# Weight preparation woven into the first two image rows, and a reordered setup, in a fused convolution, expert and recurrence kernel

## The reference

```python
# block 1: involution, 7x7 kernels made from the normalised pixel itself
w = relu(bn(conv1_w @ n1)); w = conv2_w @ w + conv2_b       # 4 groups x 49 taps
out1[c,h,w] = sum_k w[g(c),k,h,w] * patch[c,k,h,w]
# block 2: 16 experts, the top two weighted by their gates
out2 = sum_e dispatch[e] * w3[e] @ (silu(w1[e] @ n2) * (w2[e] @ n2))
# block 3: 3x3 convolution whose 64x64x9 kernel is a sum of low-rank products
y1 = conv(n3, S1s) @ U1s;  y2 = conv(n3, U2s) @ S2s;  out3 = (y1+y2)/12 + bias
# block 4: a recurrence over all 3136 pixels of an image, in row order
i,o = sigmoid(U x_t + V h); g = tanh(U x_t + V h); c = h*c + i*g; h = o*tanh(c)
```

## Time and profile before

| | us |
|---|---|
| median of three runs (4188.93 to 4189.55) | 4189.06 |
| the profiled execution | 4187.62 |
| its span, first to last instruction | 4184.9 |
| setup, to the first matmul of row 0 | 34.4 |
| rows 0 and 1 | 29.7 and 29.4 |
| preparation after row 1, after row 3 | 11.2 and 17.9 |
| from the first recurrence step to the end (3136 steps) | 3933.4 |

### The profile page before, as it was taken

The page is one execution under the profiler, slowest core; times in us unless marked ns, Lnnn a source line. Parts: engine busy times, 40 slices in busy tenths (PEclk is TensorE's granted clock), DMA queues, the critical chain, the costliest instruction groups (busy, mean ns, idle before and its releaser), DMA issues.

```text
span 4184.9 us, 135477 instructions
## 1 busy us (share of the span) xinstructions
PE 3651.3 (87%) x35548; PEld 2427.1 (58%) x35548; DVE 3452.3 (82%) x21845; ACT 2620.1 (63%) x11611; POOL 2187.3 (52%) x3228
## 2 busy tenths in 40 slices
PE   3788989898989898989898989898989898988887
PEld 2565656565656555656565655555656565655555
DVE  5678888888888888888888888888888888887777
ACT  1256666666666666666666666666666666666665
POOL 6565555555555555555554555555555555552222
PEclk9875555555555555555555555555555555555555
DMA  4000000000000000000000000000000000000000
GB/s 71 1 2 1 1 1 1 1 1 1 1 1 1 1 1 1 1 1 1 1 1 1 1 1 1 1 1 1 1 1 1 1 1 1 1 2 1 1 1 1
DMA packets 44543, 11.08 MB, mean 3 GB/s; under 512 B 39914, under 2 KB 44011, under 8 KB 44491
## 3 DMA queue, kind: packets, MB, share of 16 engines
q1 hardware_dynamic: 42378, 10.05, 1.5%
q10 hardware_dynamic: 2112, 0.46, 0.1%
HBM read 7.29 MB, written 3.21 MB: 3 GB/s over the span
## 4 chain that ended last, share of the span: by engine, by line
PE 56%; ACT 18%; DVE 18%; issue 7%; POOL 1%; SPq 0%; DVEq 0%; POOLq 0%; DMA 0%; ACTq 0%
PE GATES L1195 22%; ACT O L664 10%; PE YB L1022 8%; ACT G L661 8%; DVE HR L850 8%; DVE O L847 8%; PE YB L1162 5%; PE TAPB L1009 5%; PE DB L1130 5%; PE DB L1003 3%; PE H1B L1049 1%; PE H2B L1049 1%; PE TAPB L1054 1%; PE TAPB L1171 1%; PE GATES L992 1%
## 5 line engine op out<-in xcount | busy, mean ns | idle before, releaser
L661 ACT ACTIVATE G<-GATES 128x12 f32<-128x12 f32 x3136 | 572.7, 183 | 1254.6 <-PE GATES L1195 1198.0
L1195 PEld LDWEIGHTS GATES<-HR,VN 128*128 128x128 f16 x9408 | 496.6, 108 | 1306.1 <-DVE HR L850 1252.3
L1195 PE MATMUL GATES<-HR,VN 128*128 128x4 f16 x9408 | 758.9, 175 | 392.4 <-DVE HR L850 257.2
L842 DVE TENSOR_TENSOR_SCAN CT<-G,CT 128x12 f32<-128x12 f32 x3136 | 587.4, 187 | 306.6 <-ACT G L661 266.3
L664 ACT ACTIVATE O<-G 128x16 f32<-128x16 f32 x3136 | 690.1, 220 | 98.9 <-ACT G L661 0.2
L847 DVE RECIPROCAL O<-O 128x4 f32<-128x4 f32 x3136 | 567.4, 181 | 197.5 <-ACT O L664 0.9
L1195 PE MATMUL GATES<-H,VW 128*128 128x4 f16 x9408 | 712.9, 170 | 0.0
L850 DVE TENSOR_TENSOR_SCAN HR<-O,CT 128x20 f16<-128x20 f32 x3136 | 614.5, 196 | 4.6
L859 DVE SCALAR_TENSOR_TENSOR CT<-HIST,CT 128x4 f32<-128x4 f32 x3136 | 522.3, 167 | 108.8
L1022 PE MATMUL YB<-HD,W 128*64 128x112 f32 x3840 | 600.1, 411 | 2.4 <-DVE HD L751 2.2
L509 POOL TENSOR_TENSOR HD<-VV,DBS 128x448 f32<-128x448 f32 x392 | 444.3, 1133 | 271.3 <-ACT DBS L653 270.9
(11 more groups left out here) (236 smaller groups left out, 5588.2 us busy)
## 6 DMA issues: line engine op xcount, KB each, us to landing
out_dram<-OUT SPq DMA_DIRECT2D x112, 28.0 KB, 2.0
X<-in_x_dram SPq DMA_DIRECT2D x4, 672.0 KB, 13.4
STG<-in_L_ffn_w_dram SPq DMA_DIRECT2D x4, 512.0 KB, 8.0
U<-in_L_conv_U2s_dram SPq DMA_DIRECT2D x1, 972.0 KB
W<-in_L_ffn_w_dram SPq DMA_DIRECT2D x1, 512.0 KB, 11.5
X<-in_x_dram ACTq DMA_DIRECT2D x4, 112.0 KB, 3.0
S<-in_L_conv_S1s_dram SPq DMA_DIRECT2D x1, 108.0 KB
S<-in_L_conv_S2s_dram SPq DMA_DIRECT2D x1, 108.0 KB
```

What stands on the lines that cost most here:

```text
L661: act.activation(G6[:, :, 2:5], gates[c][:, w, :, :], ACT.Tanh, scale=1 / GSCALE).then_inc(step_in, 1)
L842: dve.tensor_tensor_scan(CELL.rearrange("z b k -> z (b k)"), G6[:, :, :].rearrange("z b k -> z (b k)")[:, 0::2], ADD3.rearrange("z b k -> ...
L1195: last = pe.matmul(gates[c][:, w, :, SLOT[g]], wt[:, g].rearrange("z m c -> z (m c)"), digit, start=False, stop=True, skip_group_check=True)
```

## The change

1. SP issues the loads first and raises the counters after the 12 smallest; the order becomes `inv_loads` (conv2 and batch norm, 6), `row_loads` (conv1, gates, 6), counters, `u_loads` (low-rank kernel, 4), experts (5), `w_loads` (20), rest of x.
2. conv2_w is replicated into `YB` instead of `DB`, before the spread of the norms, and without its wait for `RSB`. `WT` is built by VectorE (5 copies) and ACT (3 copies). GpSimd clears only two columns of `N3` and no longer all of it.
3. Rows 0 and 1 are written out on PE, ACT and VectorE in place of a loop (GpSimd keeps its loop). Their `TAPD` goes to `YB`, so that the two products of a tap row have a bank each.
4. What was done after rows 1 and 3 is put at places inside rows 0 and 1: the 45 composing matmuls (now into `DB`) on PE; `SEL`, `W3`, the high half of `WM` and of the recurrence's weights on ACT; constants, `IDUP`, the low halves and `WC` on VectorE.

```diff
+COMPOSE_AT = ({19: 4, 24: 4, 29: 4, 34: 4, 39: 4, 44: 4}, {14: 4, 19: 4, 24: 4, 29: 4, 34: 4, 39: 1})
+SEL_AT, WMHI_AT, W3S_AT, RECHI_AT, RECNEG_AT = (29, 30), (29, 30), 31, 32, 52
+CONST_AT, IDUP_AT, SELZ_AT = 30, 35, 40
+WMLO_AT, RECLO_AT, WC_AT = (33, 38, 43, 48), 49, 53
...
+        def first_taps(experts):
+            return TAPB if experts else YB
...
         def _(sp):
-            for c in counted:
-                sp.sem_inc(c, 16 if c is ostored else 2 if c is step_in else 1 + left_out.get(c, 0))
             sp.wait_ge(set_pool, 4)
             for dst, src in inv_loads:
                 sp.dma_start(dst, src).then_inc(ld_inv, 16)
+            for dst, src in row_loads:
+                sp.dma_start(dst, src).then_inc(ld_row, 16)
+            for c in counted:
+                sp.sem_inc(c, 16 if c is ostored else 2 if c is step_in else 1 + left_out.get(c, 0))
+            for dst, src in u_loads:
+                sp.dma_start(dst, src).then_inc(ld_u, 16)
             for dst, src in exp_loads:
                 sp.dma_start(dst, src).then_inc(ld_exp, 16)
+            for dst, src in w_loads:
+                sp.dma_start(dst, src).then_inc(ld_w, 16)
             for dst, src in x_loads(FIRST, H):
                 sp.dma_start(dst, src).then_inc(ld_rest, 16)
-            for dst, src in w_loads:
-                sp.dma_start(dst, src).then_inc(ld_w, 16)
...
+            for w in (0, W + 1):
+                pool.memset(N3[:, :, :, w:w + 1], 0.0)
...
-            pool.memset(N3[:, :, :, :], 0.0).then_inc(set_pool, 1)
...
+        def act_first_row(act, j):
+            for t in range(W):
+                act_fill(act, j, t, True, False, False, False)
+                if j == 0:
+                    for k, a in enumerate((0, 32)):
+                        if t == SEL_AT[k]:
+                            act.activation(SEL[a:a + 2 * E, ...], ID[...].broadcast, ACT.Copy).then_inc(set_act, 1)
+                    continue
+                for k in range(2):
+                    if t == WMHI_AT[k]:
+                        act.wait_ge(ld_exp, 16 * len(exp_loads))
+                        act.activation(WM[:, k, 0], STG[:, k], ACT.Copy, scale=WSCALE).then_inc(wm_hi, 1)
+                if t == W3S_AT:
+                    act.activation(W3[:, :, :], W3[:, :, :], ACT.Copy, scale=1.0 / WSCALE).then_inc(w3_set, 1)
+                if t == RECHI_AT:     # 8 high halves (BH, UX, VH, VW) and BX
+                    act.wait_ge(ld_w, 16 * len(w_loads))
...
+                if t == RECNEG_AT:
+                    act.wait_ge(rec_lo, 6)
+                    act.activation(VN[:, :, :, :], VW[:, :, :, :], ACT.Copy, scale=-1.0).then_inc(rec_set, 1)
...
         def _(act):
+            act.wait_ge(w2m_set, 1)
+            for g in range(1, G):
+                last = act.activation(WT[:, :, 1, g, :], W2M[:, 1, g, :]...broadcast, ACT.Copy)
+            last.then_inc(wt_set, 1)
             act.wait_ge(lead_rsb, 1)
...
-            with rows(act, 0, 2) as j:
-                act_row(act, j, True, False, False, False)
-            act.wait_ge(ld_exp, 16 * len(exp_loads))
-            for k in range(2):
-                act.activation(WM[:, k, 0], STG[:, k], ACT.Copy, scale=WSCALE).then_inc(wm_hi, 1)
+            for j in range(2):
+                act_first_row(act, j)
...
+                        if not experts and h == 0:
+                            dve.wait_ge(acc_step, 1 + ACN * j + (acc(k - 1) + 2 if k > 1 else 0))
                         dve.wait_ge(tapd_done, 1 + 2 * NT * j + 2 * k + (h + 1 if lstm else 2))
...
+        def dve_first_row(dve, j):
+            for t in range(W):
+                dve_fill(dve, j, t, True, False, False, False)
+                if j == 0:
+                    if t == CONST_AT:     # 9 linked clears: HIST G6 O5 HR H5 BX ONEH WC, O5's -1
+                    if t == IDUP_AT:      # 1 clear and 4 copies
+                    if t == SELZ_AT:
+                        dve.memset(SEL[64:128, :, :, :], 0.0).then_inc(set_act, 1)
+                    continue
+                for n in range(4):
+                    if t == WMLO_AT[n]:
+                        k, half = divmod(n, 2)
+                        e = slice(half * E // 2, (half + 1) * E // 2)
+                        dve.wait_ge(wm_hi, k + 1)
+                        dve.scalar_tensor_tensor(out=WM[:, k, 1, e], in0=STG[:, k, e], scalar=WSCALE, in1=WM[:, k, 0, e],
+                                                 op0=ALU.mult, op1=ALU.subtract).then_inc(wm_lo, 1)
+                if t == RECLO_AT:         # 12 scalar_tensor_tensor of 64 or 128 columns, no links
+                    dve.wait_ge(rec_hi, 8)
...
+                if t == WC_AT:            # the 4 copies of L971 and L973, now from DB and H2B
+                    dve.wait_ge(wc_set, 1)
...
+                    last.then_inc(h_set, 1)
...
+        def pe_first_row(pe, j):
+            n = sum(COMPOSE_AT[0].values()) if j else 0
+            for t in range(W):
+                if j == 0 and t == HEAD.DUP:
+                    pe.wait_ge(set_dve, 4)
+                pe_fill(pe, j, t, True, False, False, False)
+                if t in COMPOSE_AT[j]:
+                    if n == 0:
+                        pe.wait_ge(ld_u, 16 * len(u_loads))
+                    last = compose(pe, n, n + COMPOSE_AT[j][t])
+                    n += COMPOSE_AT[j][t]
...
         def _(pe):
+            pe.wait_ge(rep_set, 1)
+            pe.wait_ge(ld_inv, 16 * len(inv_loads))
+            pe.matmul(YB[:, 0:G * K7 * K7], REP[:, :], W2T[:, :], start=True, stop=True, ...).then_inc(set_pe, 1)
             pe.wait_ge(set_pool, 6)
             pe.wait_ge(lead_rs, RSN)
             spread_rs(pe, spread(True), 0, LEAD).then_inc(lead_rsb, 1)
...
+            for j in range(2):
+                pe_first_row(pe, j)
+            pe.wait_ge(wm_lo, 4)
+            pe.wait_ge(w3_set, 1)
+            pe.wait_ge(set_act, 3)
+            pe.wait_ge(h_set, 1)
             with rows(pe, 2, C_SKIP) as j:
                 pe_row(pe, j, True, False, True, False)
-            ... (the 45 composing matmuls)
+            pe.wait_ge(rec_set, 2)
             with rows(pe, C_SKIP, LAG) as j:
```

More of the change, by code:

```diff
@@ L675, in _ @@
             act.wait_ge(set_pool, 4)
-            act.activation(SEL[64:128, :, :, :].rearrange("z p e n -> z (p e n)"),
-                           CST[64:128, CZERO:CZERO + 1].broadcast_to([64, 2 * E * HID]), ACT.Copy).then_inc(set_act, 1)
+            act.activation(PT[:, 0:1], CST[0:TOK, CZERO:CZERO + 1], ACT.Copy)
             act.wait_ge(lead_xc, 1)
@@ L682, in _ @@
                 .then_inc(lead_ve, 1)
+            act.wait_ge(w2m_set, 1)
+            for g in range(1, G):
+                last = act.activation(WT[:, :, 1, g, :], W2M[:, 1, g, :].unsqueeze(2).broadcast_to([128, K7 * K7, GC]), ACT.Copy)
+            last.then_inc(wt_set, 1)
             act.wait_ge(lead_rsb, 1)
@@ new lines, in _ @@
+            link(dve, dve.scalar_tensor_tensor(out=W2A[:, :], in0=W2LO[:, :], scalar=MLO[:, 0:1], in1=W2A[:, :],
+                                          op0=ALU.mult, op1=ALU.add))
+            dve.tensor_scalar(W2M[:, 1].rearrange("z g k -> z (g k)"), W2A[:, :], PM[:, 1:2], None, ALU.mult).then_inc(w2m_set, 1)
+            link(dve, dve.tensor_scalar(W2M[:, 0].rearrange("z g k -> z (g k)"), W2A[:, :], PM[:, 0:1], None, ALU.mult))
+            for p, g in [(0, g) for g in range(G)] + [(1, 0)]:
+                dve.tensor_copy(WT[:, :, p, g, :], W2M[:, p, g, :].unsqueeze(2).broadcast_to([128, K7 * K7, GC]))
@@ L907, in _ @@
-            for tile_, v in ((DP, 0.0), (XS, 0.0), (HIST, 0.0), (G6, 0.0), (O5, 0.0), (HR, 0.0), (H5, 0.0), (WC, 0.0), (IDUP, 0.0), (BX, 0.0), (ONEH, 1.0)):
-                link(dve.memset(tile_[:], v))
-            link(dve.memset(O5[:, :, :, 2:3], -1.0))
-            link(dve.tensor_copy(IOT[:, :], IOTI[:, :]))
-            for p, h in enumerate(halves):
-                for d in range(2):
-                    link(dve.tensor_copy(IDUP[h, d, p, 64 * d:64 * d + 64], ID[h, h]))
-            dve.wait_ge(set_pe, 1)
@@ L1005, in spread_rs, with taps @@
             return last
-        def taps(pe, i, j0, a, b):
+        def taps(pe, bank, i, j0, a, b):
             for m in range(a, b):
-                last = pe.matmul(TAPB[:, m * TOK:(m + 1) * TOK], WT[:, i * K7 + j0 + m].rearrange("z p g c -> z (p g c)"),
+                last = pe.matmul(bank[:, m * TOK:(m + 1) * TOK], WT[:, i * K7 + j0 + m].rearrange("z p g c -> z (p g c)"),
                                  RED[:, :], start=(m == 0), stop=True, skip_group_check=True)
@@ L1112, in pe_fill @@
                 pe.wait_ge(prod_done, 1 + 2 * NT * j + 2 * k + 1)
[L1113 removed]
+                taps(pe, first_taps(experts), k, 0, 3, 4).then_inc(tapd_done, 1)
             if experts and t in P.H2:
@@ L1198, in pe_row, with compose @@
                 pe_fill(pe, j, t, involution, lstm, experts, pre)
+        def compose(pe, a, b):
```

(34 more changed lines are left out.)

208 lines of the change are left out of this document (109 added, 99 removed).

## The result

The changed kernel takes **4155.96 us** (median of 4 runs, 4155.26 to 4157.19) against 4189.0 before: ratio 0.9922, 95% interval 0.9905 to 0.9939. The forecast was 4156, range 4147 to 4167. The profiled execution took 4156.44 us with a span of 4154.7, so the span fell by 30.2. The total came out as forecast. Its terms did not: the setup gave less than I said, row 1 and its junction more, and the two partly cancel.

A forecast was written before the change was run, and what follows sets the result against it. The recurrence, 94% of the span, is unedited, so only the 251.5 us ahead of it can change. Terms -17.3 + 0.8 + 0.6 - 16.8 = -32.7 take the profiled 4187.6 to 4154.9; the median lies 1.4 higher: 4156 us, range 4147 to 4167.

The forecast's parts named there:

- Term A: Setup up to row 0's first taps: taps at 23.3 instead of 40.59, -17.3 us (-14.5 to -19.5).
- x or conv2 lands late: Rival, setup: 3136 four-byte pieces precede the rest; x landing 5 us late instead of 1 gives 4160 and more; chance 0.05.
- The step that failed outright: Setup, GpSimd: loop entry of 3.77 us from 20.1, then 1.4 of copies, ending 25.3, before its first sum at 26.0.
- straight code stalls: Rival, first rows: new code fetched late while loads fill the DMA engines, losing 4.2 and 8.6 us: 4168; chance 0.12.
- Term B: Row 0: second bank saves 0.46, compositions and ACT's work cost nothing, VectorE's blocks cost; +0.8 us (0 to +3).
- Term C: Row 1 and its junction: 3.1 lost in the row, 2.5 gained at the junction; +0.6 us (-4 to +5).
- The port: Row 1: three `WM` pieces on VectorE stop GpSimd, +3.5 less what waits anyway; together +3.1 us at the last `PD`.
- the tail: End of row 1: VectorE alone needs 9.2 us after the last `PD`, plus 3.4 for the loop: 12.6 against 15.1.
- Term D: Junction of rows 3 and 4: without compositions and copies only the 3.4 us loop entry is left; -16.8 (-15.8 to -17.8).
- Recurrence: The 3136 steps: same code, same 1.254 us a step; change 0, with 2 us for chance.
- The rival on the other side: Recurrence's loop: if one head in each of 56 passes is fetched anew, 3.2 x 56 = +179 us, 4335; chance 0.03.
- The rival of the faster PE: Rows 0 and 1: compositions make PE denser and faster, row 1 saves 2 to 3 us: 4153; chance 0.10.

The follow-up runs named there:

- the loads after x: The changed kernel with SyncE issuing its loads only after the first eight rows of x have landed; ratio 0.9903 to the kernel before.
- the counters first: The changed kernel with SyncE counting its 65 semaphores before its first load instead of after the twelfth; ratio 0.9910 to the kernel before.
- The compositions behind row 3: The changed kernel with the 45 compositions on PE and VectorE's four conv-weight copies moved back behind row 3; ratio 0.9957 to the kernel before.
- the change again: The changed kernel repeated with no edit, in another round; ratio 0.9919 to the kernel before.
- the kernel with GpSimd written out: The changed kernel with GpSimd's rows 0 and 1 written out instead of a loop of two passes; ratio 0.9907 to the kernel before.

## Why the prediction was right, and where it wasn't

**Term A, setup: -17.3 forecast, -15.75 measured at the taps and -10.9 at the first sum.** The step that failed is "I let x land 1.0 later (0 to 1.8)": it landed 3.3 later, and the loads after x and the counters first both give it back, so SP's early loads are shown as the cause. From 2 to 8 us 3642 small packets of theirs pass beside x, and conv2's 3136 pieces of four bytes are most of them; conv2's load was not moved by itself. This is half of my rival *x or conv2 lands late*, to which I gave 0.05. The parts around it held: GpSimd ahead of `RS_Y` without a wait on small loads, ACT's entry 4.2 (4.0 by itself), VectorE's five `WT` copies even faster (0.50 each instead of 0.61). The lower bound that I set, -14.5, held for the taps and not for the first sum.

**The step that failed outright** is the one on GpSimd: "still enters a loop: 3.77 from 20.1 is 23.9, and 1.4 of copies end at 25.3, 0.7 ahead of its first sum". I took a stall from one place of the trace and moved it to another as if it were a constant. It was 8.81, and the experts' weights, which now land in just these us, go with it: with them and all behind them held back it was 1.76. It cost some 4.9 us at the first sum. My rival *straight code stalls* had the right circumstance and the wrong place: an engine did stall while the loads filled the DMA engines, but in front of the one loop that was left, and nowhere in the straight rows. (Its price was added up for the profiled execution; as a median it would have been 4169, not 4168.)

**Term B, row 0: +0.8 forecast.** Measured +0.07, and +0.9 to +1.0 in the three kernels in which a single edit lets GpSimd enter early (29.2 against 28.2). The second is the term as I meant it. It is made of other parts, though: written out, the row is 1.3 shorter without any of the new work in it, so that the work costs some 2.2. The compositions are 0.3 of it.

**Term C, row 1 and its junction: +0.6 forecast, -3.1 measured.** The port was sized right: the pieces beside GpSimd cost 2.3 at the last product (3.1 forecast; 3.0 by taking them away). The Trainium skill's rule ("SBUF — State Buffer", Who interferes with whom) stands by this trace, 1.50 for a product of 0.42. What was mis-sized is the tail: VectorE needed 8.1 instead of 9.2, and the entry 1.64 instead of 3.4, near the lower end that I gave for "straight code ahead of it". That these halves bring nothing in row 1 is shown by putting them back.

**Term D, junction of rows 3 and 4: -16.8 forecast, -16.4 measured**, 3.84 left of 20.2. The compositions behind row 3 show the same from the other side.

**Recurrence: 0 forecast, +0.3 measured.** The rival on the other side, a price at every pass of the main loop, is out: one row takes 70.1 in both kernels.

**The rival of the faster PE** is out too, for rows 0 and 1. In the changed kernel their granted clock was recorded at 0.50, the lower of its two levels (1.2 GHz): it was 1.00 up to 29.5 us, and PE had no instruction in 30 to 31, where it reads 0.50. In the change again it was 1.00, the higher level (2.4 GHz), throughout both rows. The same stretch of either:

```profile
36.00:55.00 19.00, 12.99 (x80) 10.05 (x80) 12.72 (x38) 9.09 (x10) 16.53 (x24) 0.50 0.58 74
```

```profile
36.00:55.00 19.00, 12.91 (x80) 9.96 (x80) 12.80 (x38) 9.16 (x10) 16.54 (x24) 1.00 0.57 83
```

The same 80 products take PE 13.0 and 12.9. Row 0 takes 28.3 at either, and row 1 to `IXF` 32.6 at either. So PE's clock does not set these rows; the length of row 2, with the experts, goes with it.

So at the first update -32.7 was forecast and -30.6 came. A (with the late entry) lost 6.4 on the forecast, B gave 0.7 back, C 3.7, D lost 0.4, and the rest is 0.3. That the median agrees to 0.04 us is luck: the two large errors, 6.4 and 3.7, happened to have opposite signs, and four executions of the changed kernel spread over 1.9 us.

## What to carry to other kernels

A stall in front of a loop has no fixed price, so it can't be carried from one place of a trace to another. The same entry of GpSimd cost 1.5 to 1.8 us with the large loads held back and 3.8 to 9.3 beside them. Keep large loads out of the us in which an engine first enters a loop, or write the first passes out. And an earlier load is not an earlier landing: what is issued first can take time from what is needed first, as the thousands of small pieces did here.

Before two traces are compared by some us, look at the granted clock of the rows between: here the length of one and the same row went with it by 1.4 us, more than some of the edits brought.

When terms are added up, check each against its own landmark. A sum that agrees can hide two errors, and the larger one here was worth more than the term beside it.

## What the runs showed of the hardware

- An engine's entry into a loop, "issue" in the trace: GpSimd at row 0 took 8.81, 9.26 and about as much in the other kernels with the experts' loads landing, 3.77 and 4.63 in the kernels with the order of before, 1.76 and 1.54 where the experts' loads were held back, 0 without the loop. VectorE in front of row 2 took 1.2 to 2.3 where straight code came before it (none in three kernels), 3.40 behind a loop; in front of row 4 3.5 to 4.3 behind a loop, 1.73 where it had waited 14 us for PE. Loads can't be the reason there: the DMA engines' share in front of row 4 was 0.03 in the changed kernel. The main loop's entry took 3.0 to 3.7 on PE, and 3.2 and 3.3 on ScalarE behind straight code. What shortens the entry in front of row 2 was not tried by itself.
- Written-out rows showed no gap of "issue" of 1 us or more in any of these kernels, not with the DMA engines full (share 1.2 to 1.4), but for the 2.59 in front of ScalarE's first relu, which is its wait for conv1.
- 112 KB loads of x took 3.0 from issue to landing, 6.1 beside SP's small loads (3642 packets, 3136 of them conv2's).
- One execution has one pace: rows of 70.0 in one and 70.2 in another, 11 us over the recurrence, with the same instructions. What sets it, these runs don't show.
- The granted clock: row 2, looped, took 30.1 us at 1.00 and 31.5 at 0.84; rows 0 and 1 took the same at 0.50 and at 1.00.

Not tried: the counters first together with GpSimd written out, which by the two traces would bring the first taps to 21.4 and the first sum to about 24 (an estimate: 21.36, and the 2.67 between taps and first sum of the kernel with GpSimd written out).
